# Attention over 512 tokens: three PSUM banks for the transposed probabilities and three for the scores, in place of two and four

## The reference, cut to what matters

```python
logits = jnp.einsum('bhld,bhmd->bhlm', q, k) * scale + bias[None]
attn = jax.nn.softmax(logits, axis=-1)
out = jnp.einsum('bhlm,bhmd->bhld', attn, v)
```

## Time and profile before

| | us |
|---|---|
| Median of 3 runs | 2565.08 (2564.73 to 2572.67) |
| The profiled execution | 2562.15 |
| its span, first to last instruction | 2560.4 |
| attention stage, from the span's start | to about 860 |
| mean granted clock of TensorE over the span | 0.896 of 2.4 GHz |

### The profile page before, as it was taken

How to read it: one execution, slowest core, us unless ns; L and a number is a source line. 1 busy time by engine, 2 the same in 40 slices (tenths; PEclk the granted TensorE clock), 3 DMA queues, 4 the chain that set the end, 5 groups by cost and what they waited for, 6 DMA issues and landing times. The chain is left out here.

```text
span 2560.4 us, 64355 instructions
## 1 busy us (share of the span) xinstructions
PE 2086.0 (81%) x25432; PEld 1296.3 (51%) x25432; DVE 1848.1 (72%) x4475; ACT 1478.8 (58%) x4032; POOL 788.8 (31%) x851
## 2 busy tenths in 40 slices
PE   6988988988887585488888888888888884778984
PEld 2444444444444363256655555666555563555552
DVE  6777777777776335799999999899999953673333
ACT  3666766766666124357777777777777663222221
POOL 1000100100100243134444444444444431105884
PEclk7999999999998797689999999999999985788997
DMA  6000000000000431100000000000000003334334
GB/s 231 1 1 5 9 5 5 9 5 5 9 5 5 123 97 41 29 11 13 13 13 13 13 13 13 13 13 13 13 13 5 5 4 104 83 100 105 44 44 89
DMA packets 109980, 85.57 MB, mean 33 GB/s; under 512 B 22430, under 2 KB 97858, under 8 KB 109424
## 3 DMA queue, kind: packets, MB, share of 16 engines
q1 hardware_dynamic: 96112, 68.31, 9.1%
q0 software_dynamic: 13568, 13.14, 3.2%
HBM read 59.22 MB, written 22.71 MB: 32 GB/s over the span
## 5 line engine op out<-in xcount | busy, mean ns | idle before, releaser
L565 ACT ACTIVATE Pr<-Pr,nmax 128x512 f32<-128x512 f32 x512 | 341.2, 715 | 190.2 <-DVE nmax L475 187.7
L706 PE MATMUL bank<-ident,Pr 128*128 128x128 f32 x2048 | 305.6, 292 | 83.1 <-DVE PT L484 62.8
L706 PEld LDWEIGHTS bank<-ident,Pr 128*128 128x128 f32 x2048 | 234.9, 148 | 255.2 <-DVE PT L484 160.5
L475 DVE CUSTOM_DVE_ANT_0 Pr<-bank,Tb 128x512 f32<-128x512 f32 x512 | 330.9, 684 | 29.5 <-PE bank L692 28.8
L484 DVE COPY PT<-bank 128x512 f32<-128x512 f32 x256 | 176.6, 690 | 186.5 <-PE bank L720 182.9
L2469 PE MATMUL bank<-Wcv,hw 128*128 128x512 f32 x512 | 245.8, 624 | 4.9 <-ACT bank L2260 3.4
L2073 DVE TENSOR_TENSOR pr<-AC,Tc 128x30 f32<-128x30 f32 (+14 forms) x480 | 223.7, 466 | 36.0 <-POOL Tc L1946 22.2
L2074 DVE TENSOR_TENSOR Tc<-Tc,pr 128x30 f32<-128x30 f32 (+14 forms) x480 | 189.8, 395 | 16.5
L572 ACT ACTIVATE PT<-bank 128x512 f32<-128x512 f32 x256 | 150.8, 589 | 80.2 <-PE bank L720 74.1
L692 PE MATMUL bank<-kp,qp 8*128 8x512 f32 x1024 | 168.4, 661 | 0.0
L264 POOL DMA_INDIRECT disp<-H,slot x32 | 31.8, 994 | 419.6 <-DVE slot L420 354.1
(11 more groups left out here) (407 smaller groups left out, 4421.7 us busy)
## 6 DMA issues: line engine op xcount, KB each, us to landing
aB<-alpha SPq DMA_DIRECT2D x64, 128.0 KB, 2.8
Tb<-scores SPq DMA_DIRECT2D x4, 1792.0 KB, 13.2
w<-in_L_ffn_W SPq DMA_DIRECT2D x16, 256.0 KB, 5.6
rawW<-in_L_ffn_up_w SPq DMA_DIRECT2D x16, 256.0 KB, 3.2
rawW<-in_L_ffn_gw SPq DMA_DIRECT2D x16, 256.0 KB, 3.9
rawW<-in_L_ffn_down_w SPq DMA_DIRECT2D x16, 256.0 KB, 4.0
disp<-Pr SPq DMA_DIRECT2D x1, 2580.0 KB
xin<-disp SPq DMA_DIRECT2D x8, 322.5 KB, 6.2
```

The lines of the kernel that those rows point to most:

```text
L475: V.tensor_tensor_reduce(out=Pr[:, s, i, :], in0=pS[hh][:, :], in1=Tb[:, h, at:at + L], scale=-1.0, scalar=3.0e38, op0=ALU.add, op1=ALU.mi ...
L565: A_(Pr[:, s, i, :], Pr[:, s, i, :], ACT.Exp, scale=-1.0, bias=nmax[:, s, i:i + 1])\
L706: last = TR(pT[m % 2][:, t * P:(t + 1) * P], Pr[:, (G % 2) * HG + hh, t, j * P:(j + 1) * P], ident[:, :])
```

## The change

The eight banks are split in another way: three for scores, three for transposes. Scores rotate with n = 4R + hh over three banks. The score matmul n waits until VectorE has read score n - 3, so the fourth head of a round waits for the first head of the same round. The transposes rotate over three banks, and `transposes(m)` waits for the copy of m - 3. The order of the instructions on each engine stays as it was.

```diff
-        pS, pT, pO, pM = PB[0:4], PB[4:6], PB[6], PB[7]
+        pS, pT, pO, pM = PB[0:3], PB[3:6], PB[6], PB[7]
...
-                    V.tensor_tensor_reduce(out=Pr[:, s, i, :], in0=pS[hh][:, :], in1=Tb[:, h, at:at + L],
+                    V.tensor_tensor_reduce(out=Pr[:, s, i, :], in0=pS[n % 3][:, :], in1=Tb[:, h, at:at + L],
...
-                    V.tensor_copy(PT[:, m % NPS, :], pT[m % 2][:, :]).then_inc(r["b_evd"], 1)
+                    V.tensor_copy(PT[:, m % NPS, :], pT[m % 3][:, :]).then_inc(r["b_evd"], 1)
...
-                    A_(PT[:, m % NPS, :], pT[m % 2][:, :], ACT.Copy).then_inc(r["b_eva"], 1)
+                    A_(PT[:, m % NPS, :], pT[m % 3][:, :], ACT.Copy).then_inc(r["b_eva"], 1)
...
                     for hh in range(HG):
-                        if R:
-                            pe.wait_ge(r["b_s"], (R - 1) * HG + hh + 1)
+                        n = R * HG + hh
+                        if n >= 3:
+                            pe.wait_ge(r["b_s"], n - 2)
                         rows = slice(32 * hh, 32 * hh + HD0)
-                        mm(pS[hh][:, :], qp[rows, G % SLOTS, i * P:(i + 1) * P], kp[rows, G % SLOTS, :],
+                        mm(pS[n % 3][:, :], qp[rows, G % SLOTS, i * P:(i + 1) * P], kp[rows, G % SLOTS, :],
                            start=True, stop=True, tile_position=(32 * hh, 0)).then_inc(r["b_qk"], 1)
...
-                    if m >= 2:
-                        evacuated(m - 2)
+                    if m >= 3:
+                        evacuated(m - 3)
                     for t in range(LT):
-                        last = TR(pT[m % 2][:, t * P:(t + 1) * P], Pr[:, (G % 2) * HG + hh, t, j * P:(j + 1) * P],
+                        last = TR(pT[m % 3][:, t * P:(t + 1) * P], Pr[:, (G % 2) * HG + hh, t, j * P:(j + 1) * P],
                                   ident[:, :])
                     last.then_inc(r["b_pt"], 1)
```

## The result

The changed kernel takes 2852.7 us (median of 5 runs, 2832.4 to 2894.5), the kernel before 2564.7 in the same series. The ratio is 1.112, with a 95% interval of 1.108 to 1.116. The forecast was 2850 us.

A forecast was written before the change was run, and what follows sets the result against it. TensorE's order was taken to bound some rounds, VectorE's loop the others. 198 us of stall plus 88 us of lower clock, 286 us on 2562.15, made 2848 (2851 from the median); predicted 2850 us, range 2750 to 2925.

The forecast's parts named there:

- The fourth score: TensorE's scores, begun at S: fourth waits for VectorE's read until S + 1.92, transposes at S + 2.97; 1.72 us added.
- packed round: Round set by TensorE's order alone: 5.41 us before, 6.90 forecast after, 1.49 us more.
- The sum at an unchanged clock: 124 rounds with scores and transposes, half of each kind, at 1.6 us more: 198 us; bounds 185 to 208.
- late round: Round where VectorE is late and its loop, now also through score 0, sets the length: 1.68 us more.
- The third transpose bank: Second transposes before the values: 0.23 us given back per round set by TensorE, nothing else of 74.4 us of waits.
- The clock: TensorE's clock falls to 1.2 GHz in two rounds of three, 1.5 us a fall: 88 us; bounds 0 to 150.
- B: Rival: the fourth score's stall with today's clock, 2750 to 2800 us; chance 0.24.
- E: Rival: no change, the 124 stalls are paid by waits that exist; chance 0.01.
- C: Rival: TensorE's clock falls nearly every round, 2900 to 2960 us; chance 0.2.
- D: Rival: faster, fourth score's wait costs nothing and the added transpose bank removes 74.4 us: 2491 us; chance 0.03.
- The Trainium skill: PSUM bank rule: one of four heads follows with one more pair of passes, 130 us, so 2695 us in all.
- passes of heads 0 to 2 are not held up by the waiting fourth: Sign at the scores: were they held up, VectorE starting head 0 after S + 1.16, the prediction would be wrong.

The follow-up runs named there:

- The later profile: The changed kernel unaltered, run and profiled once more in a later series: 2871.9 us, ratio 1.122; the profiled execution took 2876.6 us.
- the late order: The changed kernel with the fourth score of a round issued after the values in place of right behind the third: 2563.0 us, ratio 1.001.

## Why the prediction was right, and where its terms were off

*The fourth score.* Right to a hundredth of a microsecond in a packed round: S + 2.96 for 2.97. A packed round lasts 6.89 us where 6.90 was forecast (411.40 to 418.29 in the timeline of the changed kernel; 5.41 before). Adding the wait alone and taking its place in the order away show it from both sides: 2957.9 us and 2563.0.

*The sum at an unchanged clock.* This term, 198 us, was mis-sized. It can be read from the rounds themselves. Of the 123 rounds from the fifth on, 37 ran at 2.4 GHz throughout both before and after. There the changed kernel's round is longer by 1.17 us on average (by -0.14 to 1.57), where the prediction had 1.49 for a packed round and 1.68 for a late one. The later profile gives 1.17 again, over 39 rounds. The kernel with four filling transposes gives 1.30 over 75 rounds. At 1.17 to 1.30, the 124 rounds cost 145 to 161 us.

The step that failed is the late round. The prediction let VectorE's loop set it, 1.68 us longer. In the changed kernel TensorE's own order is so long that VectorE is seldom late: the fourth score starts at S + 1.91, as in a packed round, in at least half of the rounds at 2.4 GHz. A wait that a round had before, for a copy of VectorE or of ScalarE, then passes while TensorE does its longer work, and has to be taken off the price of the step. One round with a short piece of `misc`, before and after:

```profile
523.77 1.25 PE L692 MATMUL bank<-kp,qp 8*128 8x512 f32 x8
525.19 1.06 PE L706 MATMUL bank<-ident,Pr 128*128 128x128 f32 x8 [0.17 <-DVE PT L484]
...
528.06 1.09 PE L706 MATMUL bank<-ident,Pr 128*128 128x128 f32 x8 [0.25 <-DVE PT L484]
529.09 1.31 PE L692 MATMUL bank<-kp,qp 8*128 8x512 f32 x8
```

```profile
714.60 1.13 PE L693 MATMUL bank<-kp,qp 8*128 8x512 f32 x6
716.51 1.12 PE L693 MATMUL bank<-kp,qp 8*128 8x512 f32 x2 [0.78 <-DVE nmax L475]
...
720.05 1.07 PE L707 MATMUL bank<-ident,Pr 128*128 128x128 f32 x8
721.05 1.32 PE L693 MATMUL bank<-kp,qp 8*128 8x512 f32 x5
```

It lost 6.45 - 5.32 = 1.13 us. A round with a key projection waits for ScalarE's copy before, and lasts 463.82 - 457.93 = 5.89 us:

```profile
457.93 1.31 PE L692 MATMUL bank<-kp,qp 8*128 8x512 f32 x8
459.17 0.66 PE L706 MATMUL bank<-ident,Pr 128*128 128x128 f32 x4
460.33 0.66 PE L706 MATMUL bank<-ident,Pr 128*128 128x128 f32 x4 [0.50 <-ACT PT L572]
...
463.82 1.31 PE L692 MATMUL bank<-kp,qp 8*128 8x512 f32 x8
```

The same round after the change lasts 626.43 - 619.53 = 6.90 us, and that wait is gone:

```profile
619.53 1.31 PE L693 MATMUL bank<-kp,qp 8*128 8x512 f32 x6
...
622.50 1.09 PE L707 MATMUL bank<-ident,Pr 128*128 128x128 f32 x8
...
626.43 1.31 PE L693 MATMUL bank<-kp,qp 8*128 8x512 f32 x6
```

This round lost 1.01 us. With the third bank taken back it lasts 631.15 - 624.26 = 6.89 us and has no such wait either, so here the longer order took the wait away, and not the bank.

*The third transpose bank.* The prediction credited "none of the 74.4 us apart from the 0.23" of a packed round, 14 us if half of the rounds are packed. The runs give the bank 33 to 52 us behind the fourth score's wait and 38 without that wait.

*The clock.* The direction was right and the size too low. From the windows, (1 - 0.92) x 2 x 786 = 126 us of the rounds ran at 1.2 GHz before and 487 us after, 361 more. At the 0.36 to 0.45 us that the comparisons above give for each, that is 130 to 162 us of the 320 in the profiled execution, which leaves 158 to 190 for the stall. The other runs had the higher clock; with 0.861 over a span of 2850.9 us, (1 - 0.861) x 2 x 2850.9 = 792 us ran low, against 533 before (0.896 over 2560.4). At 0.36 to 0.45 that is 93 to 117 us of the 288, and 171 to 195 for the stall. The rounds at 2.4 GHz, above, say 145 to 161 for the stall, which leaves 127 to 143 for the clock; the rounds with a lower clock in either trace are not in that reading. The prediction had 198 and 88. By either reading the stall was taken too large and the clock too small, so much of the closeness of 2850 to 2853 is luck; how the 288 us divide within these bounds is open. What the clock follows is shown as far as this: filling the gap before the fourth score brought it from 0.82 to 0.92, with four transposes as with seven. The idle time in sum does not decide: TensorE stood still for 84 of the 695 us before, at a clock of 0.94, and for 80 after, at 0.82. Nor does the lone score by itself: with the fourth score late it still runs alone, but TensorE stands still for 6 us only, and the clock is 0.96. So the gap before the fourth score has a part in it, since filling it helped; whether its length, its place or the company of matmuls of 8 rows counts for more is open.

*Rivals.* B, today's clock, falls with that, and E, no change, with the result; C, a fall in nearly every round, would have given over 2900. D, faster, needed VectorE to be through with head 0 before head 3's turn; that is what the late order gives it, and even then three score banks only come level.

*The Trainium skill* is cited in the prediction, TensorEngine Tiling (Array Packing), section Gotcha 1: PSUM Pressure, for its rule that different row tiles write different PSUM banks. With the row's 1.05 us the prediction estimated 130 us for a follower alone. The late order shows that cost by itself (1.05 us a round); the wait on VectorE comes on top.

## What to carry to other kernels

Where matmuls of a few rows run side by side in strips of the array, a ring of banks shorter than the set makes the last one wait for a reader of the same round, and run alone; price both before taking a bank away. When a step makes one engine's order longer, look which waits of today pass behind it, and take them off its price. Before giving a ring another buffer, read which release ends its wait: here it was the slot of a copy's output, and one more slot, or the consumer moved ahead, gave 4.4%. A gap of 0.6 to 0.8 us in every round cost here 93 to 143 us through TensorE's clock, about as much as by its own length (0.87 us in each of 124 rounds, 108 us).

## What was not expected of the hardware

- Work added to TensorE made the kernel faster: four useless transposes a round, 2792.9 us against 2871.9.
- The clock's share differs between kernels with nearly equal rounds: 0.79 and 0.74, 53 us apart in their medians.
- The prediction took without a row that passes of heads 0 to 2 are not held up by the waiting fourth, and the trace bears it out: six L693 passes run from 425.27, both of each head, 1.91 us before the fourth's two.
